# Forming the first chunk's degrees between the sums of the first source tiles of layer 1

## The chip, the cores and the metric

The kernel runs on one core of a Trainium2 chip. The metric is the device time of one execution in microseconds (us). Engines: PE is TensorE's matmul, PEld its weight load, DVE VectorE, ACT ScalarE, POOL GpSimd, SP SyncE, which here only issues DMAs.

## The reference

Four layers of a graph network over 3125 nodes and 50000 edges, with a layer norm and a relu ahead and the input added at the end. Each layer averages over a node's incoming edges; the divisor is the node's degree, at least one.

```python
def _sage_conv(x, src, dst, Wl, Wr, b):
    agg = jax.ops.segment_sum(x[src], dst, num_segments=n)
    deg = jax.ops.segment_sum(jnp.ones_like(dst, dtype=x.dtype), dst, num_segments=n)
    mean = agg / jnp.maximum(deg, 1.0)[:, None]
    return mean @ Wl + x @ Wr + b
h = jnp.maximum(_layernorm(x, axis=-1), 0.0)
h = jax.nn.relu(_sage_conv(h, src, dst, Wl1, Wr1, b1))
h = jax.nn.relu(_sage_conv(h, src, dst, Wl2, Wr2, b2))
h = jax.nn.relu(_sage_conv(h, src, dst, Wl3, Wr3, b3))
return x + _sage_conv(h, src, dst, Wl4, Wr4, b4)
```

## The kernel before

**The matrix of edge counts.** The sum over edges is a product with a matrix `counts`: row = source node, column = destination node, value = how many edges join them. It stays in SBUF as 25 source tiles (NT) of 128 rows, in f16. The destinations are worked through in 7 chunks (NCH), six of 512 nodes (4 tiles each, TPC) and one of 53. `ORDER` begins with chunk 5, then the chunk of 53, then 4, 3, 2, 1, 0. "q" is the place in that order, so q = 0 is chunk 5.

**How the matrix is made.** It is built during the kernel. A *step* is one product of PE (`step`, L2183) of two one-hot tables, which adds up to 128 edges to a window of destinations in PSUM (`window_ps`). DVE makes the tables in *groups*: for windows of 8 nodes, three steps to a group, with two instructions each (L1479); for the narrower windows of 4 nodes four steps to a group, one instruction (L1472). There is room for three groups; DVE reuses the oldest when PE is through with it. When a pair of windows is full ACT copies it to `counts` (L1876), and the next window that wants the bank waits for that copy (`window_stored`). Before layer 1 begins the matrix holds chunk 5 only. The rest is made between layer 1's sums.

**Layer 1's place q = 0.** The list `script(0)` gives the order in which PE, DVE and ACT go through this place: for each of the 25 source tiles k a first half of the sum ("sum"), then a second half ("half"), and after each half two or three steps. A half is two products of 512 columns (`add_sources`, L2362), one for the high and one for the low part of the sources. On every engine other work hangs on the numbers k in a table called `first_round`: on DVE the moments, shifts and low parts of the layer norm of the chunks still to come (`h0_moments`, `h0_shift`, `h0_low_part`) and tables of edges (`bases_late`, `late_rows`); on PE the transposes of normalized inputs (`h0_turn(j)`, L2128) and their product with Wr1 (`own_products(j)`, L2140), both through the PSUM banks `lin_ps`; on ACT the roots and the copies. Each engine runs its own list in order, and semaphores join them.

**The degrees.** Ahead of the first half PE forms the degrees of chunk 5 (`add_degrees(0)`, L2384): for each of its 4 tiles of destinations, 25 products of `counts` (as weights, 128 x 128) with two columns of ones, 100 in all, into eight columns of `lin_ps`. DVE then takes the maximum with one and the reciprocal (`degrees(0)`, L1616 and L1618), and `degree_inverted` tells PE that these columns have been read. `h0_turn(2)`, PE's first use of `lin_ps` after that, waits for it; PE issues it ahead of source tile 4. The turned degrees are used after tile 24. Place q = 2 forms its 100 products in the same way, ahead of its sums (L2384 too).

**The start of q = 0.** PE comes to it from the last steps of chunk 5 once ACT has copied the last window, after a loop over windows with unusually many edges (`heavy_of`). DVE comes to it from the same loop and first does `h0_moments(3)` and `bases_late(2)`, which hang on tile 0, and then the first two groups of tables. SP waits for the first product of the first sum (`chunk_begun`) and then issues a small copy within SBUF and the stores of the turned inputs.

Of the kernel before, what the change touches and what calls it, by code (L numbers as in the profile page):

```python
# [26 lines left out]
def sage_stack_kernel(nc, x, src, dst, Wl1, Wr1, b1, Wl2, Wr2, b2, Wl3, Wr3, b3, Wl4, Wr4, b4, out):  # L27
# [14 lines left out]
    P = 128  # L42
# [3 lines left out]
    NT = -(-N // P)  # L46
    TAIL = N - (NT - 1) * P
    TPC = 4
# [59 lines left out]
    ORDER = [NFULL - 1, NFULL] + list(range(NFULL - 2, -1, -1))  # L108
# [59 lines left out]
    for at_, (w, i) in enumerate(STEP):  # L168
        if i:
            continue  # L170
        k = STEPS[w]
# [8 lines left out]
    BY_STEPS = 3  # L180
# [87 lines left out]
    with ctx:  # L268
# [10 lines left out]
        counts = sb("counts", [P, NT, NPAD], f16)  # L279
# [77 lines left out]
        ones16 = upper[:, NWIN:NWIN + P]  # L357
# [139 lines left out]
        lin_ps = pb("lin_ps", [P, 2, 512], f32)  # L497
# [70 lines left out]
        own_copied = sem("own_copied")  # L568
# [9 lines left out]
        degree_done = sem("degree_done")  # L578
# [142 lines left out]

        assert len(FILLS[-1]) == 32 and BY_STEPS == 3
        IN_LIN = 5
        FIRST_J, FILL_J = 3, 2
        LAST_DEGREE_TURN_K = 22
        H0_LATE_K, OWN_LATE_K = 1, (4, 5)
# [441 lines left out]
        def _(dve):  # L1168
# [29 lines left out]
            def h0_moments(j):  # L1198
                c = ORDER[j]
                n, t = size_of(c)  # L1200
                dve.wait_ge(x_loaded[c], 16 if n == CH else 32)
                if j > 0:
                    dve.wait_ge(moments_made, BEFORE[j])
                for i in range(t):
                    order.after(v.bn_stats(stats[:, i, :], x_in[c][:, i, :])) if i == t - 1 else v.bn_stats(
                        stats[:, i, :], x_in[c][:, i, :])
                for i in range(t):
                    v.bn_aggr(moments[c][:, i, :], stats[:, i, :]).then_inc(moments_made, 1)
# [16 lines left out]
            def h0_low_part(j):  # L1225
                c = ORDER[j]
                n, t = size_of(c)
                tiles = slice(c * TPC, c * TPC + t)
                dve.wait_ge(h0_high, j + 1)
                if n == CH:  # L1230
                    v.scalar_tensor_tensor(out=H[:, tiles, 1, :], in0=x_in[c][:, 0:t, :], scalar=0.0,
                                           in1=H[:, tiles, 0, :], op0=ALU.max, op1=ALU.subtract).then_inc(h0_low, 1)
                else:
                    twin = slice(TWIN, P)
                    v.scalar_tensor_tensor(out=H[twin, tiles, 0, :], in0=x_in[c][twin, 0:t, :], scalar=0.0,
                                           in1=H[twin, tiles, 0, :], op0=ALU.max, op1=ALU.subtract).then_inc(h0_low, 1)
# [29 lines left out]
            def bases_late(piece):  # L1266
                if piece == 2:
                    dve.wait_ge(lo_made, 3)
                bases(piece, base_late[piece - 2], PIECES[piece][0])
                if piece == 3:  # L1270
                    dve.sem_inc(bases_made, 1)
# [340 lines left out]
            def degrees(q):  # L1612
                n, t = size_of(chunk_at(q))
                rows_ = P if n == CH else n
                dve.wait_ge(degree_done, q + 1)
                order.after(v.tensor_scalar(rdeg_columns[0:rows_, q, 0:t], lin_ps[0:rows_, 0, 0:2 * t].rearrange(  # L1616
                    "p (t a) -> p t a", a=2)[:, :, 0], 1.0, None, ALU.max))
                v.reciprocal(rdeg_columns[0:rows_, q, 0:t], rdeg_columns[0:rows_, q, 0:t]).then_inc(degree_inverted, 1)  # L1618
# [7 lines left out]
            for i, w in enumerate(FILLS[-1]):  # L1626
                if i in between:
                    between[i]()
                for j in range(steps_of([w])):
# [1 line left out]
            load_heavy(dve, regs, 0)  # L1631
            dve.wait_ge(consts_made, CONSTS)
            heavy_of(-1)
            first_round = {0: lambda: (h0_moments(3), bases_late(2)), 1: lambda: (degrees(0), h0_low_part(2)),
                           3: lambda: bases_late(3), 5: lambda: (late_rows(), h0_shift(3)), 7: lambda: h0_shift(4),
                           9: lambda: h0_low_part(3), 10: lambda: square_weights(), 11: lambda: late_tables(2),
                           12: lambda: h0_low_part(4), 13: lambda: h0_shift(5), 15: lambda: h0_low_part(5),
# [419 lines left out]
        def _(pe):  # L2057
# [292 lines left out]
            def add_sources(l, q, bank, k, first, final, halves=None):  # L2350

                c = chunk_at(q)
                n, t = size_of(c)
                if l == 1:
                    k = TILES[k]
                rows_, parts = (STACK, 1) if k == NT - 1 else (P, 2)
                if l == 1 and k == NT - 1:
                    pe.wait_ge(tail_doubled, 16 * (q + 1))
                tile = H_tiles(l, k, 1)[0:rows_, 0, :, :]
                for h in halves or range(AGG[l]):  # L2360
                    for part in range(parts):
                        last = m((agg_ps, window_ps)[bank][:, h, 0:n], tile[:, part, h * P:(h + 1) * P],  # L2362
                                 counts[0:rows_, k, chunk_cols(c, n)], start=first and part == 0,
                                 stop=final and part == parts - 1)
                        if l == 1 and first and h == 0 and part == 0:
                            last.then_inc(chunk_begun, 1)
                    if final:
                        last.then_inc(agg_done[l], 1)

            def add_degrees(q):  # L2370

                c = chunk_at(q)
                n, t = size_of(c)
                rows_ = P if n == CH else n
                if q == 0:
                    pe.wait_ge(own_copied, 2 * FILL_J)
                elif q == 1:
                    pe.wait_ge(own_copied, 2 * IN_LIN)
                else:
                    pe.wait_ge(low_done[1], q - 1)  # L2380
                for i in range(t):
                    for k in range(NT):
                        of = slice(0, TAIL if k == NT - 1 else P)
                        last = m(lin_ps[0:rows_, 0, 2 * i:2 * i + 2], counts[of, k, bass.ds((c * TPC + i) * P, rows_)],  # L2384
                                 ones16[of, 0:2], start=(k == 0), stop=(k == NT - 1))
                last.then_inc(degree_done, 1)

            def sum_cuts(q):

# [55 lines left out]
            for q in range(NCH):  # L2445

                if q == 2:
                    load_heavy(pe, regs, 1)
                    pe.wait_ge(step_tables, 5)
                pe.wait_ge(window_stored, filled_after(q - 1))  # L2450
                if q < BY_STEPS:
                    add_degrees(q)
                else:
                    if q < NCH - 1:
                        sum_cuts(q)
                    pe.wait_ge(low_done[1], q - 1)
                for kind, k in script(q):
                    if kind == "step":
                        step(*k)
                    if kind == "half":  # L2460
                        if k == 0 and q >= 1:
                            pe.wait_ge(agg_scaled[1], 2 * q)
                        add_sources(1, q, 0, k, k == 0, k == NT - 1, halves=(1,))
                    if kind == "lin":
                        lin_part(q - 1, k)
                    if kind == "narrow":
                        narrow_part(q - 1, k)
                    if kind != "sum":
                        continue
                    if k == 2 and 0 < q < BY_STEPS:  # L2470
                        pe.wait_ge(degree_inverted, q + 1)
                    if k == CUT_SUM_K and q == NCH - 1:
                        sum_cuts(q)
                    if q == 0 and k in LOW_AT:
                        pe.wait_ge(h0_low, LOW_AT[k])
                    if q == 0 and k in first_round:
                        first_round[k]()
                    if q == 1 and k == H0_LATE_K:
                        for j in range(IN_LIN + 1, NCH):
                            h0_turn(j)  # L2480
                    if q == 1 and k in OWN_LATE_K:
                        own_products(IN_LIN + OWN_LATE_K.index(k))
                    if q == 1 and k == TURN_K:
                        pe.wait_ge(own_copied, 2 * NCH)
                    if k == 0 and q >= 1:
                        pe.wait_ge(agg_scaled[1], 2 * q - 1)
                    add_sources(1, q, 0, k, k == 0, k == NT - 1, halves=(0,))
                    if k == (NT, LAST_DEGREE_TURN_K, DEGREE_TURN_K, NT, NT, NT, NT)[q]:
                        turn_degrees(q)
                    if q >= 1 and k == TURN_K:  # L2490
                        turn(1, q - 1, 0)
                if q == 0:
                    pe.wait_ge(rdeg_made, 1)
                    pe.wait_ge(norms_made, 3)
                    h0_turn(IN_LIN)
                heavy_of(q)
# [105 lines left out]
```

## Time and profile before

| | |
|---|---|
| median of 3 executions | 645.88 us (645.56 to 646.54) |
| profiled execution, its own time | 645.63 us |
| its span, first to last instruction | 643.8 us |
| outside the span | 1.8 us |
| PE busy | 615.5 us, 96% of the span |
| DVE busy | 318.9 us, 50% |
| ACT busy | 194.1 us, 30% |
| mean granted clock of TensorE | 0.986 of full |

Times inside the profile count from the span's start. A granted clock of 1.00 is the upper of TensorE's two levels, 2.4 GHz, and 0.50 the lower, 1.2 GHz. PE busy has to be read with care: it is also "busy" while its products run at the lower level.

### The profile page before, as it was taken

What the parts mean: (1) busy time and instruction counts of PE and PEld (TensorE: products, weight loads), DVE (VectorE), ACT (ScalarE), POOL (GpSimd) and SP (SyncE); (2) the same over time, 40 slices, a digit from 0 to 9 for tenths busy, and PEclk for the clock granted to TensorE, in tenths of its full rate; (3) what the DMA queues carried; (4) which work ended last, traced back from release to release, by engine and by line L of the source; (5) the groups of instructions that cost most, each with busy time, mean ns of one, the idle gap of its engine ahead of it and who ended that gap; (6) DMA issues with size and microseconds to landing.
All of it is one profiled execution on the core that took longest, in us unless ns stands there. A gap on an engine that the chain in (4) does not pass through costs nothing.

```text
span 643.8 us, 10273 instructions
## 1 busy us (share of the span) xinstructions
PE 615.5 (96%) x4155; PEld 339.3 (53%) x4156; DVE 318.9 (50%) x616; ACT 194.1 (30%) x411; POOL 41.8 (6%) x91
## 2 busy tenths in 40 slices
PE   5678999999999999999999999999999999999998
PEld 4435555656555555554444445444445646556586
DVE  6977876878888779721211111111126343334421
ACT  3876866365653622300111001122122010000100
POOL 8001300000000000000000000000002020110110
PEclk9977999999999999999999999999999999999999
DMA  8401200510210202142433531534451133030330
GB/s 265 104 1 46 85 1 3 184 57 6 68 53 15 88 23 83 34 139 67 147 89 89 151 86 50 106 98 111 140 126 33 43 86 113 2 115 10 105 116 33
DMA packets 59687, 51.00 MB, mean 79 GB/s; under 512 B 31670, under 2 KB 44507, under 8 KB 59640
## 3 DMA queue, kind: packets, MB, share of 16 engines
q1 hardware_dynamic: 59284, 49.74, 26.8%
q8 instruction: 33, 0.54, 0.3%
q0 software_dynamic: 240, 0.37, 0.2%
q10 hardware_dynamic: 116, 0.24, 0.1%
q14 instruction: 14, 0.11, 0.1%
HBM read 28.15 MB, written 16.60 MB: 70 GB/s over the span
## 4 chain that ended last, share of the span: by engine, by line
PE 86%; DVE 6%; ACT 3%; DMA 2%; issue 2%; POOL 1%; SPq 0%; DVEq 0%; ACTq 0%; POOLq 0%
PE agg_ps L2362 34%; PE window_ps L2362 19%; PE lin_ps L2297 5%; PE window_ps L2183 5%; PE lin_ps L2246 3%; PE lin_ps L2140 2%; PE agg_ps L2338 2%; PE lin_ps L2266 2%; PE lin_ps L2305 2%; DVE early L1479 1%; PE lin_ps L2384 1%; PE degree_ps L2061 1%; PE turn_ps L2183 1%; PE window_ps L2338 1%; ACT counts L1876 1%
## 5 line engine op out<-in xcount | busy, mean ns | idle before, releaser
L2362 PE MATMUL agg_ps<-counts,H 128*128 128x512 f16 (+2 forms) x1026 | 235.1, 355 | 1.0 <-DVE aggT L1570 0.8
L2362 PEld LDWEIGHTS agg_ps<-counts,H 128*128 128x128 f16 (+1 forms) x1026 | 79.2, 98 | 56.2 <-issue 10.2
L1876 ACT ACTIVATE counts<-window_ps 128x400 f16<-128x400 f32 x150 | 73.5, 506 | 62.8 <-PE window_ps L2183 49.7
L1472 DVE TENSOR_TENSOR counts<-early 128x2048 f16<-128x2048 bf16 x66 | 78.0, 1213 | 7.2 <-PE window_ps L2183 4.8
L2362 PE MATMUL window_ps<-counts,early 128*128 128x512 f16 (+2 forms) x346 | 77.8, 379 | 0.0
L2362 PEld LDWEIGHTS window_ps<-counts,early 128*128 128x128 f16 (+1 forms) x346 | 33.5, 98 | 41.3 <-issue 3.4
L2362 PE MATMUL window_ps<-counts,H 128*128 128x512 f16 (+1 forms) x291 | 55.2, 346 | 0.0
L2183 PEld LDWEIGHTS window_ps<-counts 128*128 128x128 f16 x412 | 30.9, 99 | 33.2 <-issue 4.6
L1472 DVE TENSOR_TENSOR early<-early 128x1024 f16<-128x1024 bf16 (+1 forms) x69 | 43.9, 684 | 7.6 <-PE window_ps L2183 6.1
L2362 PE MATMUL agg_ps<-counts,early 128*128 (+4 forms) x297 | 46.5, 314 | 0.0
L2183 PE MATMUL window_ps<-counts 128*128 128x100 f16 x412 | 41.4, 210 | 1.0 <-DVE counts L1472 0.8
L1926 ACT ACTIVATE newT<-newT,columns 128x512 f32<-128x512 f32 (+1 forms) x21 | 13.4, 663 | 90.6 <-DVE newT L1754 66.2
L1134 POOL TENSOR_TENSOR newH<-newH,plan 128x256 f32<-128x256 f32 (+1 forms) x25 | 18.3, 760 | 334.2 <-DMA newH<-in_x_dram 334.2
L2183 PE MATMUL window_ps<-early 128*128 128x100 f16 (+1 forms) x256 | 33.1, 229 | 7.0 <-DVE early L1479 5.3
L2362 PEld LDWEIGHTS window_ps<-counts,H 128*128 128x128 f16 x291 | 24.7, 97 | 28.6 <-issue 1.1
L2183 PEld LDWEIGHTS window_ps<-early 128*128 128x128 f16 x256 | 21.7, 102 | 33.7 <-ACT counts L1876 6.9
L1570 DVE SCALAR_TENSOR_TENSOR aggT<-agg_ps,columns,rdeg 128x512 f32<-128x512 f32 (+1 forms) x21 | 13.7, 679 | 46.5 <-PE agg_ps L2362 43.4
L2362 PEld LDWEIGHTS agg_ps<-counts,early 128*128 128x128 f16 (+1 forms) x297 | 22.0, 97 | 24.3 <-issue 1.1
L1923 ACT ACTIVATE newT<-lin_ps,columns 128x512 f32<-128x512 f32 (+1 forms) x14 | 10.1, 723 | 66.8 <-PE lin_ps L2297 62.5
L2039 ACT ACTIVATE H<-selfT 128x512 f16<-128x512 f32 (+1 forms) x12 | 6.1, 557 | 70.5 <-DMA selfT<-hT_d 70.5
L1591 DVE SCALAR_TENSOR_TENSOR partsT<-newT,partsT 128x512 f16<-128x512 f32 (+1 forms) x9 | 5.3, 587 | 44.1 <-ACT partsT L1940 43.9
L2246 PE MATMUL lin_ps<-aggT,W 128*128 128x512 f32 (+1 forms) x56 | 25.1, 564 | 0.6 <-DVE aggT L1570 0.6
(302 smaller groups left out, 712.5 us busy)
## 6 DMA issues: line engine op xcount, KB each, us to landing
selfT<-hT_d SPq DMA_DIRECT2D x18, 512.0 KB, 4.2
hT_d<-newT SPq DMA_DIRECT2D x12, 512.0 KB, 4.6
rdeg<-rdeg_d SPq DMA_DIRECT2D x22, 256.0 KB, 4.1
counts<-in_x_dram SPq DMA_DIRECT2D x6, 512.0 KB, 8.1
hT_d<-counts SPq DMA_DIRECT2D x6, 512.0 KB, 3.6
newH<-in_x_dram SPq DMA_DIRECT2D x6, 512.0 KB
out_dram<-newT SPq DMA_DIRECT2D x5, 512.0 KB
hT_d<-newT SPq DMA_DIRECT2D x6, 256.0 KB, 3.8
```

The costliest lines, as they stand in the source:

```text
L1134: nc.gpsimd.tensor_tensor(x4[0:q, i, :], x4[0:q, i, :], b4rows[0:q, :], ALU.add).then_inc(x4_biased, 1)
L1472: v.tensor_tensor(hots_of(group).rearrange("p r a (n d) -> p r a n d", d=2), pairs.unsqueeze(1).unsqueeze(1).broadcast_to([P, n, 2, P // 2 ...
L1570: v.scalar_tensor_tensor(out=aggT[:, h, 0:n], in0=(agg_ps, window_ps)[bank][:, h, 0:n], scalar=SPLIT if l == 4 else unscale[:, l - 1:l], i ...
L1876: a.activation(counts[:, :, 2 * w * WIN:2 * (w + 1) * WIN].rearrange("p t (a w) -> p a t w", a=2), window_bank(FILL_AT[w])[:, 0:2 * KEYS]. ...
L1926: a.activation(newT[:, h, 0:n], source, ACT.Relu, bias=bT[:, bias + h:bias + h + 1]).then_inc(relu_done[l], 1)
L2140: last = m(h0_ps(j)[h][:, 0:n], W14[:, 1, k, h * P:(h + 1) * P], x_T[c][:, k, 0:n], start=(k == 0), stop=(k == 1))
L2183: m(window_bank(at)[:, key0:key0 + keys], one_src, one_key, start=(j == 0), stop=(j == STEPS[w] - 1)).then_inc(hot_used, 1)
L2246: last = m(lin_ps[:, h, 0:n], W14[:, 0, k, h * P:(h + 1) * P], aggT[:, k, 0:n], start=(k == 0), stop=(k == 1))
L2266: m(last_ps(i)[0:rows_, 0:D], h, w, start=(j == 0), stop=(j == len(products) - 1))
L2297: last = m(lin_ps[:, h, 0:n], w, r, start=(i == 0), stop=(i == len(ops) - 1))
L2338: last = m((agg_ps, window_ps)[bank][:, h, cols], tile[:, part, h * P:(h + 1) * P], counts[0:rows_, k, c * CH + g * HALF_CH:c * CH + (g + ...
L2362: last = m((agg_ps, window_ps)[bank][:, h, 0:n], tile[:, part, h * P:(h + 1) * P], counts[0:rows_, k, chunk_cols(c, n)], start=first and p ...
```

## The change

The 100 products of chunk 5's degrees no longer stand ahead of the first sum. Each of the first eight halves of sums (source tiles 0 to 3, two halves each) is followed by 13 of them (the eighth by the last 9), ahead of that half's steps. They are the same products into the same columns in the same order. The wait for `own_copied` moves with them, behind the first half. On DVE `degrees(0)` moves from tile 1 to tile 4, since its inputs are complete only after tile 3. `add_degrees` for q = 1 and q = 2 is as before.

```diff
+        FIRST_DEGREES = 13
...
-            first_round = {0: lambda: (h0_moments(3), bases_late(2)), 1: lambda: (degrees(0), h0_low_part(2)),
+            first_round = {0: lambda: (h0_moments(3), bases_late(2)), 1: lambda: h0_low_part(2), 4: lambda: degrees(0),
...
-                if q == 0:
-                    pe.wait_ge(own_copied, 2 * FILL_J)
-                elif q == 1:
+                if q == 1:
                     pe.wait_ge(own_copied, 2 * IN_LIN)
...
+            def add_first_degrees(slot):
+
+                c = ORDER[0]
+                if slot == 0:
+                    pe.wait_ge(own_copied, 2 * FILL_J)
+                for at in range(FIRST_DEGREES * slot, min(FIRST_DEGREES * (slot + 1), TPC * NT)):
+                    i, k = at // NT, at % NT
+                    of = slice(0, TAIL if k == NT - 1 else P)
+                    last = m(lin_ps[:, 0, 2 * i:2 * i + 2], counts[of, k, bass.ds((c * TPC + i) * P, P)],
+                             ones16[of, 0:2], start=(k == 0), stop=(k == NT - 1))
+                    if at == TPC * NT - 1:
+                        last.then_inc(degree_done, 1)
...
-                if q < BY_STEPS:
+                if 0 < q < BY_STEPS:
                     add_degrees(q)
-                else:
+                elif q > 0:
...
                         add_sources(1, q, 0, k, k == 0, k == NT - 1, halves=(1,))
+                        if q == 0:
+                            add_first_degrees(2 * k + 1)
...
                     add_sources(1, q, 0, k, k == 0, k == NT - 1, halves=(0,))
+                    if q == 0:
+                        add_first_degrees(2 * k)
```

Lines of the changed kernel are numbered 2 higher from DVE's part on (13 to 17 higher after the new function's place). The next rows are PE's program at the start of q = 0 before the change; `lin_ps<-newH,counts 128x2` are the degrees' products (`newH` holds the ones), `agg_ps` a half of a sum, `window_ps` the steps.

```order
L2236 ISA
L2384 MATMUL lin_ps<-newH,counts 128x2 x100
L2362 MATMUL agg_ps<-counts,H 128x512 x2
L2183 MATMUL window_ps<-early 128x200 x3
L2362 MATMUL agg_ps<-counts,H 128x512 x2
L2183 MATMUL window_ps<-early 128x200 x2
```

And the same place in the changed kernel:

```order
L2238 ISA
L2364 MATMUL agg_ps<-counts,H 128x512 x2
L2396 MATMUL lin_ps<-newH,counts 128x2 x13
L2185 MATMUL window_ps<-early 128x200 x3
L2364 MATMUL agg_ps<-counts,H 128x512 x2
L2396 MATMUL lin_ps<-newH,counts 128x2 x13
L2185 MATMUL window_ps<-early 128x200 x2
```

Between PE's arrival and its first three steps there stood 100 small products and one half of a sum; now there stand 13 and one half.

The end of the products in the changed kernel, ahead of `h0_turn(2)` (L2130, eight transposes into `lin_ps`), on PE:

```order
L2364 MATMUL agg_ps<-counts,H 128x512 x2
L2396 MATMUL lin_ps<-newH,counts 128x2 x9
L2185 MATMUL window_ps<-early 128x100 x2
L2130 MATMUL lin_ps<-newH,counts 128x128 x8
L2364 MATMUL agg_ps<-counts,H 128x512 x2
```

Before, tile 3 ended with the same half, steps and transposes without the 9 products between them.

DVE's program before the change, from the second group of tables on (L1231 is `h0_low_part(2)`, L1276 `late_rows`, L1222 the last part of `h0_shift(3)`; the ten small instructions of `bases_late(3)`, L1250, stand between the third and fourth of the blocks here and are left out):

```order
L1479 TENSOR_TENSOR early<-early 128x600
L1616 TENSOR_SCALAR newH<-lin_ps 128x4
L1618 RECIPROCAL newH<-newH 128x4
L1231 SCALAR_TENSOR_TENSOR H<-counts,H 128x4x256
...
L1472 TENSOR_TENSOR early<-early 128x1024 x2
L1276 TENSOR_SCALAR counts<-degree_ps 128x6
```

In the changed kernel, the two pieces that answer to these:

```order
L1481 TENSOR_TENSOR early<-early 128x600
L1233 SCALAR_TENSOR_TENSOR H<-counts,H 128x4x256
...
L1474 TENSOR_TENSOR early<-early 128x1024
L1618 TENSOR_SCALAR newH<-lin_ps 128x4
L1620 RECIPROCAL newH<-newH 128x4
L1474 TENSOR_TENSOR early<-early 128x1024
L1278 TENSOR_SCALAR counts<-degree_ps 128x6
```

The two instructions of `degrees(0)` now stand behind `bases_late(3)` and one group of tables, with the next group, `late_rows` and `h0_shift(3)` queued behind them. The programs of ACT, POOL and SP are unchanged.

## Rows read from the trace of the kernel before

**Rows 1.** The page: span, and each engine's busy time
```profile
span 643.8 us, 10273 instructions
PE 615.5 (96%) x4155; PEld 339.3 (53%) x4156; DVE 318.9 (50%) x616; ACT 194.1 (30%) x411; POOL 41.8 (6%) x91
```

**Rows 2.** The chain that ended last: start us, us, what
```profile
49.83 0.77 issue
50.60 3.30 PE lin_ps L2384 x100
53.90 0.97 PE agg_ps L2362 x2
54.87 0.50 PE window_ps L2183 x3
...
61.25 0.43 PE agg_ps L2362 x2
61.77 0.89 PE lin_ps L2128 x8
```

**Rows 3.** Granted clock by windows (PEclk stands third from the end)
```profile
52.00:53.00 1.00, 1.00 (x33) 0.94 (x30) 1.00 (x4) 0.58 (x2) 0.00 (x0) 0.80 0.00 0
53.00:54.00 1.00, 1.00 (x27) 0.93 (x27) 0.23 (x2) 0.14 (x1) 0.00 (x0) 0.50 0.00 0
...
59.00:60.00 1.00, 1.00 (x6) 0.44 (x5) 0.85 (x5) 0.23 (x1) 0.00 (x0) 0.79 0.15 41
```

**Rows 4.** The degrees' products alone, two windows at either clock
```profile
51.00:51.50 0.50, 0.50 (x20) 0.47 (x17) 1.00 0.00 0
53.00:53.50 0.50, 0.50 (x20) 0.50 (x20) 0.50 0.00 0
```

**Rows 5.** DVE's timeline: start us, us, instruction [idle before <-releaser]
```profile
50.97 0.77 DVE L1250 TENSOR_TENSOR counts<-counts 98x128 f16<-98x128 f16 x5
51.78 1.39 DVE L1479 TENSOR_TENSOR early<-early 128x384 f16<-128x384 bf16 x4
53.94 0.16 DVE L1616 TENSOR_SCALAR newH<-lin_ps 128x4 f32<-128x4 f32 x1 [0.77 <-PE lin_ps L2384]
54.23 1.19 DVE L1231 SCALAR_TENSOR_TENSOR H<-counts,H 128x1024 f16<-128x1024 f32 x1
...
60.72 0.16 DVE L1276 TENSOR_SCALAR counts<-degree_ps 128x6 int32<-128x6 f32 x1
...
61.20 1.38 DVE L1222 TENSOR_SCALAR counts<-counts,newH 128x256 f32<-128x256 f32 x4
62.50 1.93 DVE L1472 TENSOR_TENSOR early<-early 128x1024 f16<-128x1024 bf16 x3
```

**Rows 6.** PE's timeline before, at and after the degrees
```profile
48.29 0.34 PE L2183 MATMUL agg_ps<-early 128*128 128x200 f16 x2 [0.29 <-ACT counts L1876]
...
61.60 1.06 PE L2128 MATMUL lin_ps<-newH,counts 128*128 128x128 f32 x8
...
63.97 0.30 PE L2183 MATMUL window_ps<-early 128*128 128x100 f16 x3
```

**Rows 7.** ACT's timeline at the start of q = 0
```profile
53.85 0.30 ACT L1824 ACTIVATE newH<-counts 128x4 f32<-128x4 f32 x1 [1.27 <-issue]
55.24 0.50 ACT L1876 ACTIVATE counts<-window_ps 128x400 f16<-128x400 f32 x1 [1.09 <-PE window_ps L2183]
```

**Rows 8.** PE's timeline: the same products at place q = 2
```profile
124.14 3.22 PE L2384 MATMUL lin_ps<-newH,counts 128*128 128x2 f16 x100
```

**Rows 9.** Granted clock behind those products, as in rows 3
```profile
127.00:128.00 1.00, 1.00 (x16) 0.59 (x13) 0.97 (x6) 0.00 (x0) 0.00 (x0) 0.84 0.66 131
...
131.00:132.00 1.00, 1.00 (x11) 0.63 (x10) 0.00 (x0) 0.68 (x2) 0.00 (x0) 0.95 0.11 30
```

**Rows 10.** The edge tables' gathers (POOL) and PE's first use of them
```profile
61.77 1.18 POOL L1119 DMA_INDIRECT counts<-edge_rows,counts  x1 [46.83 <-DVE counts L1276]
...
71.67 0.32 PE L2090 MATMUL degree_ps<-ident,counts 128*128 128x128 f16 x3
```

More of the change, by code:

```diff
@@ L723, in sage_stack_kernel @@
         IN_LIN = 5
+        FIRST_DEGREES = 13
+        assert 8 * FIRST_DEGREES >= TPC * NT
         FIRST_J, FILL_J = 3, 2
```

## The prediction

> **What bounds the kernel now.** I read the page first: PE is busy 96% of the span, every other engine half of it or less [rows 1]. So what counts is what PE does without working, and at which clock it works. Then the chain that ended last, from the arrival at q = 0 on [rows 2]: it runs through PE alone. PE starts the 100 small products at 50.60, needs 3.30 us, and goes from there to sums, steps and the transposes of `h0_turn(2)` at 61.77 (the chain dates a matmul's end a little later than the timeline, which has them at 61.60 [rows 6]). No wait for another engine stands between. Third, the granted clock [rows 3]: PE was idle from 48.6 (the end of the last step, 48.29 and 0.34 [rows 6]) to 50.6, then had two us of two-column products, and at about 52.6 the clock went to the lower level (0.80 over the window 52 to 53). It came back at about 59.4 (0.79 over 59 to 60). From 53.9 to 59.3, 5.4 us, the sums and steps ran at half speed, which costs half of that, 2.7 us.
>
> Last the lists of the engines that PE will meet earlier: DVE [rows 5] and ACT [rows 7]. DVE is the important one. Until 51.74 it makes `bases_late(2)`, from 51.78 to 53.17 the first two groups of tables. Today nobody notices, since PE wants the first group only at 54.66, behind the products and half a sum.
>
> **The change part by part.** *The products themselves.* 100 in 3.30 us is 33 ns each [rows 2]. They take the same at either clock: a half us at 1.00 and one at 0.50 hold the same count, 20 with those cut by its edges [rows 4]. So PE's work on them stays 3.3 us, 0.42 us for 13. Nothing is removed. The first load of weights in each slot can go beside the sum ahead of it, but the step behind the slot loses the same cover, since two columns hide nothing; I take the net as nothing. The trace has no such mixture; the bounds are eight loads more or fewer, 8 x 33 ns = 0.26 us either way.
>
> The Trainium skill, "TensorE: Matmul & The Clock Gate", section "Step-by-step: what each phase is for", says that weights for the next product are loaded while the present one runs. By that alone the eight slots would save 0.26 us; the same rule takes it back at the step behind, which had that cover before.
>
> *Wait 1, the first tables.* The sum's first half now starts at 50.60, at the full clock, 0.43 us (a later half at full clock, 61.25 [rows 2]). With 13 products PE is at its first step at 51.45. The tables are four instructions in 1.39 us from 51.78, so the first group is there at 52.48 [rows 5], whatever PE does: what stands ahead of it on DVE doesn't wait for the sums. PE waits 1.05 us. Behind that wait stands everything PE has. The wait was covered by the 87 products that have gone.
>
> *Wait 2, the copy.* ACT is occupied until 54.15 with the root of `h0_root(3)` (53.85 and 0.30, after 1.27 us without a releaser) and only then copies the first windows, 0.50 us [rows 7]. The third pair of windows, five steps in, needs that bank: PE comes to it at about 54.4, the copy is done at 54.7. 0.25 us.
>
> *Wait 3, the reciprocals.* `h0_turn(2)` needs `degrees(0)`, and DVE can begin it only at product 100, which is now two steps ahead of the transposes. Maximum and reciprocal take from 53.90 to about 54.3 [rows 2, 5]: 0.4 us, of which the steps cover 0.09. I take 0.35 us. Before, the transposes came seven us later.
>
> *Wait 4, what is queued behind `degrees(0)`.* DVE has a group of tables (0.64 us), `late_rows` and the small instructions of the shift (60.72 to 61.20, 0.48), the shift (61.20 to 62.50, 1.30) and then the group for the 24th step (0.64) [rows 5], in all 3.06 us from the reciprocal. Before, DVE began this before PE got to the transposes. PE wants that group 63.97 - 61.60 = 2.37 us after the start of the transposes [rows 6], which is at the reciprocal too. 0.7 us, and with the semaphores 0.75.
>
> Together 1.05 + 0.25 + 0.35 + 0.75 = 2.4 us. Above that I see nothing late: the product of layer 1's own weights behind gives DVE 3.5 us to catch up. The gathers on POOL wait for `late_rows` (L1276), so they start some 2 us later too, but 61.77 to 71.67 is far more than they need ahead of PE's use of them, and PE's use moves with them [rows 10]. SP's copy and stores wait for the first product of the sum and come 3.3 us earlier; no wait in the chain here is for them.
>
> *What the clock gives back.* The small products don't slow down at the lower clock, so it pays to have them there. PE's two us of idleness before 50.6 remain and it does even less up to 52.5, so I expect the fall at about 52.6 again. If the clock returns at 59.3 as before, the 6.7 us between hold four slots of products (52 x 33 ns = 1.7 us) and wait 2 (0.25), and 4.75 us of sums and steps instead of 5.4. That is 0.65 us less at half speed: 0.3 us back. The first half sum at full clock is within this.
>
> **Sum:** 2.4 - 0.3 = +2.1 us on the profiled execution's own 645.63, which is 647.7. The median of the runs shown stands 0.25 us above that execution, so a median could as well be 647.9; I keep 647.7.
>
> **The rivals.** *The clock returns early.* Mixed products, steps and sums may be enough for an earlier return. The nearest rows: at q = 2 it fell at 127.7, at the end of 3.2 us of small products, and was back at 131.0 after 3.4 us of sums and steps [rows 8, 9]. If it is back at 56.0, 3.4 us after its fall, only 3.4 - 0.25 - 0.85 = 2.3 us of sums and steps are slow, 3.1 less than before, 1.55 us saved: +0.85, 646.5. Against it: at q = 0 it took from 52.6 to 59.4 [rows 3], with small products only at the beginning; now they are all along.
>
> *The clock returns late.* It may not return at all while small products are mixed in: at the lower clock they are a quarter of PE's time (0.42 beside 0.85 of sum and 0.17 to 0.50 of steps). Then PE crawls through all of them, to about 64.1, and needs 3.4 us of dense work after it as at q = 2 [rows 8, 9], so returns at 67.5. Between 52.6 and 67.5 lie 14.9 - 0.6 (waits 2 and 3) - 2.8 (87 products) = 11.5 us of slow work against 5.4, 3.05 us more. Wait 4 goes, because a slow PE lets DVE catch up: 1.65 + 3.05 = +4.7, 650.3. For it: both returns in the rows came only after 3.4 to 5.4 us with nothing but sums and steps.
>
> *The clock doesn't fall, so that the kernel is not slower.* The half sum at 50.6 now stands in the stretch that ended in the fall. If that and the mixture behind it keep the clock up, all 2.7 us of slow work are saved against 2.4 us of waits: -0.3, 645.3. It decides at a price of 2.4: at most 0.6 us of slow work may be left. Against it: PE idles from 48.6 to 50.6 and again, by wait 1, from 51.45 to 52.5; only 0.43 us of dense work stand between.
>
> The Trainium skill's same page, section "What's actually happening", says of the monitor behind the clock that it is free-running and "doesn't reset when your kernel starts". By that, executions of one kernel would differ in where the clock falls and returns, and a median mixes the cases above. The one trace here can't show it; the three times lie 1 us apart, which would fit.
>
> *The waits aren't there.* For this DVE would have to reach the tables sooner. Its first row here starts when PE's loop is over, as before, so I see no way.
>
> **How the numbers follow.** A measurement of this kernel can tell 0.2%, 1.3 us, from no change: slower begins at 647.2, faster ends at 644.6. Waits with a return between 57 and 61: 0.50, between +1.4 and +2.9 (647.0 to 648.5; the 0.26 of either sign is in it). Early return: 0.20, 646.3 to 647.0. Late return: 0.22, 649.3 to 650.6. Clock stays up: 0.06, 645.0 to 645.9. Something else that makes it faster: 0.02. The likeliest is the first, 647.7, its own range 647.0 to 648.5. For 8 in 10 I leave out the upper half of the late return and the cases with the clock up: 646.3 to 650.0. Slower by over 0.2%: 0.45 of the first and the late return, 0.67. Same: the rest of the first, the early return, the clock that stays up: 0.30. Faster: 0.03.
>
> **What would show it.** Wait 1: PE's first three steps wait for DVE's L1481 for about 1 us, to 52.5. Wait 3: `h0_turn(2)` waits for L1620. Wait 4: PE's next steps wait for L1474 for 0.7 us. The products: 13 in about 0.42 us, and the steps behind them without a gap. The clock: its windows between 52 and 68 say which case it is. If PE has no wait at 51.5, or the steps behind the slots start late by more than a weight load, or the clock keeps its full level, the prediction is wrong in that step. Behind 75 us everything should be shifted as a whole.

## The result

The changed kernel takes 652.59 us in the median of 4 executions (651.32 to 653.73), the kernel before 646.21 us beside it on the same chip (4 executions, 645.56 to 647.79). The ratio is 1.0102, with a 95% interval of 1.0077 to 1.0126: slower by 6.4 us. Forecast were 647.7, with 646.3 to 650.0 as the range for 8 in 10. The direction was right; two thirds of the loss were not foreseen.

The page of the changed kernel, profiled in an execution of 651.32 us (lines of the changed kernel are numbered 2 higher than in rows 1 to 10 up to `add_sources`, L2364; the degrees' products are now L2396):

```profile
span 649.5 us, 10273 instructions
PE 618.6 (95%) x4155; PEld 341.6 (53%) x4156; DVE 319.0 (49%) x616; ACT 194.1 (30%) x411; POOL 42.4 (7%) x91
```

PE is busy 3.1 us longer with the same 4155 products than in [rows 1], and has 2.6 us more time without any.

**Where the time lies.** All three engines load the list of windows with many edges (`heavy`) into registers just ahead of q = 0, and again at q = 2. The two loads cut the kernel into three parts. One row for each kernel, of before and of after: engine, operation, count, duration in ns (lowest, middle, highest), start of the first and of the last in us.

```profile
L1154 DVEq TENSOR_LOAD <-heavy x2: 981/985/989, 47.6 to 123.3; - x2
```

```profile
L1156 DVEq TENSOR_LOAD <-heavy x2: 976/984/993, 47.4 to 128.8; - x2
```

Between the loads lie 75.7 us before and 81.4 after, 5.7 more. Ahead of the first there are 47.6 and 47.4, behind the second 520.5 and 520.7 of the spans. So in these two profiles everything happened in the stretch with the change, and nothing was given back or lost later. I call this stretch M and quote it for every experiment, since it leaves out the part ahead of the first load, which took between 47.4 and 49.4 us in the profiled executions, whatever the edit. A fall of the clock behind the degrees' products of q = 2 lies behind M.

PE's timeline after, from its arrival on (idle time before, and its releaser, in brackets):

```profile
50.48 0.59 PE L2364 MATMUL agg_ps<-counts,H 128*128 128x512 f16 x2 [2.05 <-ACT counts L1878]
50.91 0.47 PE L2396 MATMUL lin_ps<-newH,counts 128*128 128x2 f16 x13
52.47 0.66 PE L2185 MATMUL window_ps<-early 128*128 128x200 f16 x3 [1.09 <-DVE early L1481]
52.92 1.06 PE L2364 MATMUL agg_ps<-counts,H 128*128 128x512 f16 x2
53.77 0.71 PE L2396 MATMUL lin_ps<-newH,counts 128*128 128x2 f16 x13
54.34 0.33 PE L2185 MATMUL window_ps<-early 128*128 128x200 f16 x1
56.48 0.35 PE L2185 MATMUL window_ps<-early 128*128 128x200 f16 x1 [1.81 <-ACT counts L1878]
...
64.32 0.45 PE L2396 MATMUL lin_ps<-newH,counts 128*128 128x2 f16 x9
64.70 0.26 PE L2185 MATMUL window_ps<-early 128*128 128x100 f16 x2
65.44 1.92 PE L2130 MATMUL lin_ps<-newH,counts 128*128 128x128 f32 x8 [0.48 <-DVE newH L1620]
...
69.48 0.29 PE L2185 MATMUL window_ps<-early 128*128 128x100 f16 x3
```

There are three waits, 1.09 + 1.81 + 0.48 = 3.38 us. The second is the one that was put at 0.25. Its history is in the chain that ended last (start, us, what; "ACTq" is ACT's sequencer, which handles register instructions):

```profile
52.21 0.19 ACT counts L1817
52.40 0.02 issue
52.42 2.97 ACTq L1156
...
55.73 0.30 ACT newH L1826
56.03 0.40 ACT counts L1878
56.43 0.05 issue
56.48 0.35 PE window_ps L2185
```

Before, the chain went through PE alone here [rows 2]. Now it goes through ACT, and in ACT through one register load, L1156 (L1154 before). The same load in the two kernels, on ACT:

```profile
L1154 ACTq TENSOR_LOAD <-heavy x2: 902/908/914, 52.6 to 123.7; - x2
```

```profile
L1156 ACTq TENSOR_LOAD <-heavy x2: 919/1944/2968, 52.4 to 129.3; - x2
```

It begins at about the same time but takes 2.97 us in place of 0.90; the one at q = 2 still takes 0.92. What has moved beside it are SP's DMAs. Before:

```profile
54.47 0.68 SPq L858 DMA_DIRECT2D counts<-counts  x1
55.20 1.27 SPq L812 DMA_DIRECT2D hT_d<-counts  x2
```

After, with the windows of their transfers (the last two columns are the DMA engines' busy share and GB/s, the one ahead of them the granted clock):

```profile
50.89 0.68 SPq L860 DMA_DIRECT2D counts<-counts  x1
51.62 1.27 SPq L814 DMA_DIRECT2D hT_d<-counts  x2
```

```profile
52.00:53.00 1.00, 0.53 (x4) 0.51 (x5) 1.00 (x4) 0.40 (x2) 0.00 (x0) 0.50 0.10 26
53.00:54.00 1.00, 1.00 (x10) 0.44 (x9) 1.00 (x1) 0.00 (x0) 0.00 (x0) 0.50 0.83 298
54.00:55.00 1.00, 0.67 (x13) 0.39 (x10) 1.00 (x4) 0.00 (x0) 0.00 (x0) 0.50 0.77 254
```

SP is released by the first product of the first sum. That product no longer has 100 small ones ahead of it, so the stores start 3.6 us sooner and lie in the middle of ACT's load. Behind the load ACT has the root of `h0_root(3)` (55.73, before 53.85 [rows 7]) and the first copy of windows, for whose bank PE waits.

**The clock.** It fell at about 51.8 (0.91 over the window 51 to 52), came back at 62.0, and fell once more from 65.5 to 68.9, behind the wait for the reciprocals. Before it was low once in this stretch, from 52.6 to 59.4 [rows 3]: 6.8 us then, 13.6 now.

```profile
51.00:52.00 1.00, 0.38 (x14) 0.29 (x12) 0.96 (x7) 0.94 (x5) 0.00 (x0) 0.91 0.00 0
...
62.00:63.00 1.00, 1.00 (x23) 0.87 (x22) 0.00 (x0) 0.97 (x4) 0.00 (x0) 0.97 0.00 0
...
65.00:66.00 1.00, 0.56 (x3) 0.59 (x4) 0.96 (x5) 0.50 (x1) 0.00 (x0) 0.74 0.00 0
...
68.00:69.00 1.00, 1.00 (x6) 0.51 (x5) 0.74 (x2) 0.00 (x0) 0.80 (x1) 0.56 0.29 66
```

Of the 13.6 us, 0.7 are the end of wait 1, 1.8 wait 2, and 1.6 are four slots of small products, which don't care. The other 9.5 us were sums, steps and transposes at half speed, against 5.4 before: 4.1 more, half of which is 2.05 us. Waits of 3.4 us and 2.05 us of slower work make 5.45 of the 5.7 us of M; 0.25 us are left for everything else, the joints of the slots among it.

### The profile page after: what moved, and what is told of

Same layout as the page of the kernel before. It is cut to its first block, busy times and chain, and to the rows that moved or that the text cites. A ratio compares the mean times of both kernels' runs of the same rounds, so it can differ in the third digit from the quotient of the medians.

```text
span 649.5 us, 10273 instructions
## 1 busy us (share of the span) xinstructions
PE 618.6 (95%) x4155; PEld 341.6 (53%) x4156; DVE 319.0 (49%) x616; ACT 194.1 (30%) x411; POOL 42.4 (7%) x91
## 4 chain that ended last, share of the span: by engine, by line
PE 85%; DVE 6%; ACT 3%; DMA 2%; issue 2%; POOL 1%; ACTq 0%; SPq 0%; DVEq 0%; POOLq 0%
PE agg_ps L2364 34%; PE window_ps L2364 19%; PE lin_ps L2299 5%; PE window_ps L2185 5%; PE lin_ps L2248 3%; PE lin_ps L2142 2%; PE agg_ps L2340 2%; PE lin_ps L2268 2%; PE lin_ps L2307 1%; PE turn_ps L2185 1%; DVE early L1481 1%; PE degree_ps L2063 1%; PE window_ps L2340 1%; ACT counts L1878 1%; PE lin_ps L2270 1%
## 5 line engine op out<-in xcount | busy, mean ns | idle before, releaser
L2364 PE MATMUL agg_ps<-counts,H 128*128 128x512 f16 (+2 forms) x1026 | 236.2, 356 | 3.0 <-ACT counts L1878 2.0
L2364 PEld LDWEIGHTS agg_ps<-counts,H 128*128 128x128 f16 (+1 forms) x1026 | 79.3, 99 | 58.5 <-issue 12.4
L2364 PE MATMUL window_ps<-counts,early 128*128 128x512 f16 (+2 forms) x346 | 77.7, 379 | 0.0
L2364 PEld LDWEIGHTS window_ps<-counts,early 128*128 128x128 f16 (+1 forms) x346 | 33.5, 98 | 41.2 <-issue 3.4
L2364 PE MATMUL window_ps<-counts,H 128*128 128x512 f16 (+1 forms) x291 | 55.2, 346 | 0.0
L2364 PE MATMUL agg_ps<-counts,early 128*128 (+4 forms) x297 | 46.5, 314 | 0.0
L2364 PEld LDWEIGHTS window_ps<-counts,H 128*128 128x128 f16 x291 | 24.7, 97 | 28.6 <-issue 1.1
L2364 PEld LDWEIGHTS agg_ps<-counts,early 128*128 128x128 f16 (+1 forms) x297 | 22.1, 97 | 24.3 <-issue 1.1
```

## The experiments

"Held" in what follows means: the changed kernel with the edit of e1. My theory was that the stores beside ACT's load cost most of what was not foreseen; the rivals were that the waits for tables and reciprocals, or the clock alone, do it. Numbers of before beside the experiments: 646.35 (e1 to e4), 645.74 (e5 to e8), 646.29 us (e9 to e12), 15 or 29 executions each.

**e1: after, with SP held until ACT's fourth root.**

```diff
                 if l == 1:
+                    sp.wait_ge(root_made, 4)
                     double_tail(0)
```

> The changed kernel, and SP waits for ACT's root of chunk place 3 before it issues its copy and stores of q = 0, so they come after ACT's register load instead of beside it. Theory A (the stores, started 3.6 us earlier by the change, slow ACT's register load from 0.9 to 3.0 us, and PE waits 1.8 us for ACT's copy): the load is back at 0.9 to 1.0 us, PE's wait for the copy falls from 1.8 to at most 0.4 us, and the time is 1.4 to 2.5 us under the changed kernel's. Theory B (the load is slow for another reason, PE's or DVE's earlier work): the load stays near 3 us, the time within 0.5 us of the changed kernel's.

Measured: 647.95 us (12 executions), ratio 1.0031 [1.0014, 1.0048]. 4.6 of the 6.4 us are gone, more than the 1.4 to 2.5 expected, which counted the wait and left out the clock. M is 77.5. PE's waits, and ACT's root (lines one higher again):

```profile
52.51 0.66 PE L2186 MATMUL window_ps<-early 128*128 128x200 f16 x3 [1.16 <-DVE early L1482]
62.95 1.06 PE L2131 MATMUL lin_ps<-newH,counts 128*128 128x128 f32 x8 [0.48 <-DVE newH L1621]
65.79 0.29 PE L2186 MATMUL window_ps<-early 128*128 128x100 f16 x3 [0.31 <-DVE early L1475]
```

```profile
53.70 0.30 ACT L1827 ACTIVATE newH<-counts 128x4 f32<-128x4 f32 x1 [1.27 <-issue]
```

The wait for ACT isn't there, the root is back in its place, and the low clock is 6.8 us as before (51.9 to 58.7). What is left is what had been forecast: waits of 1.16, 0.48 and 0.31 us, and a time near 647.7. One of the twelve executions took 652.09 us, with a mean clock of 0.979 against 0.987 to 0.989 in the others.

**e2: before, with SP released by the first product of the degrees** (the collision without the change). It drops the release behind the first sum of q = 0 and adds:

```diff
+                        if q == 0 and i == 0 and k == 0:
+                            last.then_inc(chunk_begun, 1)
```

> The kernel before, but SP is let go by the first of the 100 degree products instead of the first product of the sum, 3.3 us earlier, as in the changed kernel; nothing else moves. Theory A: ACT's register load takes 2.5 to 3 us here too; ACT then copies the first pair of windows at 56.0 to 56.5 instead of 55.2, PE waits up to 0.5 us for it, and the time is 0 to 1 us over before. Theory B: the load stays at 0.9 us, no change.

Measured: 646.62 us (12), ratio 1.0001 [0.9989, 1.0012], M 75.9. ACT's load took 3.08 us, and PE waited 0.39:

```profile
L1154 ACTq TENSOR_LOAD <-heavy x2: 892/1984/3076, 54.0 to 125.3; - x2
```

```profile
58.14 0.35 PE L2183 MATMUL window_ps<-early 128*128 128x200 f16 x1 [0.39 <-ACT counts L1876]
```

So the slow load comes from the stores and not from the changed order of PE. With 100 products ahead of the sum it lies almost wholly under PE's work and costs nothing that can be measured. The collision costs time only together with the change's loss of cover.

**e3: after, with two slots of 50 products** (`FIRST_DEGREES = 50`).

> The changed kernel with 50 products behind each of the first two halves instead of 13 behind each of eight. Theory A with the waits of the prediction: the 50 products take 1.6 us and cover the wait for the first tables (1.1 us) and most of the wait for ACT's copy (1.8 us to at most 0.5), the waits at the reciprocals (0.5 us) go as well, and there is no second fall of the clock: 4 to 6 us under the changed kernel, about the kernel before (within 1 us). A rival: the interleaving as such costs (slots of products run slower than in one piece, the clock falls whenever they stand between sums): then at most half of the 6 us comes back.

Measured: 647.61 us (12), ratio 1.0017 [1.0005, 1.0029], M 77.2. The 37 products more ahead of the first steps cover wait 1 whole; the load still takes 2.98 us, PE waits 0.64 for ACT. 5.0 us came back, as expected, but the median is 1.3 over before and not within 1. The clock didn't fall a second time, as expected, but it was low for 10.2 us against 6.8 before, and for 6.8 against 3.4 at q = 2, in the profile.

**e4: after, with `bases_late(2)` on DVE behind the first tables** (the wait for tables removed alone).

```diff
-            first_round = {0: lambda: (h0_moments(3), bases_late(2)), 1: lambda: h0_low_part(2), 4: lambda: degrees(0),
+            first_round = {0: lambda: h0_moments(3), 1: lambda: (bases_late(2), h0_low_part(2)), 4: lambda: degrees(0),
```

> The changed kernel, with bases_late(2) on DVE moved from tile 0 to tile 1, behind the first two groups of tables. The wait of PE for the first tables falls from 1.1 to 0.3 us. If waits add up, the time falls by 0.7 us. If ACT's copy is what PE waits for next whatever the tables do (ACT is held until 56.0 by its register load), PE only waits 0.8 us longer there and the time stays within 0.3 us of the changed kernel's; I expect this.

Measured: 653.91 us (6), ratio 1.0103 [1.0084, 1.0122], M 82.4, with low clock for 17.1 us in the profile against 13.6 in after: nothing gained.

```profile
53.59 0.42 PE L2185 MATMUL window_ps<-early 128*128 128x200 f16 x3 [0.33 <-DVE early L1481]
58.48 0.35 PE L2185 MATMUL window_ps<-early 128*128 128x200 f16 x1 [3.36 <-ACT counts L1878]
```

The wait for tables shrank to 0.33 us and the wait for ACT grew from 1.81 to 3.36: PE only came sooner to the same late copy. While the load is slow, no cost of wait 1 shows.

**e5: held, with two slots of 50** (e1 and e3 together).

> The changed kernel with both: SP's copy and stores held until ACT's root, and 50 products behind each of the first two halves. If the two remedies are for different waits (theory A), PE has no wait left between 50.5 and 70 and the time is 0.3 to 1.5 us under two slots alone, within 0.5 us of the kernel before. If holding the stores only helps because it shortens a stretch that two slots shorten too, the time equals two slots alone.

Measured: 646.68 us (11), ratio 1.0004 [0.9992, 1.0017]. No wait of PE between its first sum and `own_products(2)`, low clock 6.8 us, M 75.5 against 75.7. The change is back at the time of before once both covers are.

**e6: after, with the small copy early and only the stores held.**

```diff
                     double_tail(0)
+                    sp.wait_ge(root_made, 4)
                     for j in range(3):
```

> The changed kernel, SP's small copy within SBUF (53 KB) as early as there, but the three stores behind it held until ACT's root. If the big stores are what slows ACT's register load, the load takes 0.9 to 1.2 us and the time is that of the kernel with both held (1.3 to 2 us over before). If the small copy does it, the load stays at 3 us and the time at 6 us over before. I expect the first.

Measured: 652.03 us (4), ratio 1.009 [1.0058, 1.0121].

```profile
L1157 ACTq TENSOR_LOAD <-heavy x2: 902/1086/1271, 54.1 to 131.0; - x2
```

The load took 1.27 us and PE's wait for ACT's copy is 0.3 us, so it is the two stores (512 and 53 KB) that make the load slow; the load beside the copy within SBUF alone (53 KB) was 0.37 us longer than before's 0.90. The time stayed high all the same, and the expectation, which had it lower, was missed there: the clock was low for 17.1 us in the profile (54.1 to 71.2), and M is 81.4. The mean clocks of the four were 0.989 (648.2 us), 0.982 (651.4), 0.976 (652.7) and 0.979 (653.1). The execution at the high clock is at e1's time, the others at that of after. So a load that is nearly quick again is not enough to bring the time back; the clock has to return early too.

**e7: held, four slots of 25.**

> The changed kernel, copy and stores held, 25 products behind each of the first four halves. The products end at tile 1, so the waits for the reciprocals (0.5 us) and for the tables behind them (0.3 us) go, and the first tables are waited for 0.75 instead of 1.15 us. By the waits alone: 1.2 us under the kernel with the stores held and thirteen to a slot, that is 0.4 us over the kernel before. If mixing products with sums costs by itself, by the clock, it stays 1 us or more over before.

Measured: 649.73 us (5), ratio 1.0067 [1.0053, 1.0081], M 77.5. A wait for the tables of 0.78 us, as expected, and low clock of 10.2 us at q = 0 with 6.8 at q = 2 where before has 3.4. By the waits it should have been 0.4 us over before; it is 4.0 over, so here the rival came true: the clock costs what the waits give back. All five executions had a mean clock of 0.981 or 0.982.

**e8: held, the first steps one source tile later**, with `h0_low_part(2)` on DVE behind them (`FIRST_STEPS_K = 1`).

> The changed kernel, copy and stores held, and the steps of q = 0 begin at tile 1 instead of tile 0, with h0_low_part(2) on DVE at tile 2. PE has 1.7 us of sums and products before it needs the first tables, so wait 1 (1.15 us) falls to under 0.3 us. Waits 3 and 4 stay or grow by 0.3 us. If waits add up: 0.8 to 1.1 us under the kernel with the stores held. If the clock, low in either, hides it: under 0.4 us.

Measured: 653.38 us (4), ratio 1.0126 [1.0111, 1.0142], M 81.9. It should have been about 1 us under e1 and is 5.4 over it. Wait 1 was gone, but steps that begin a tile later come more to a half, and PE waited for copies (1.31 and 0.43 us) and later for tables (1.33); the clock was low for 10.2 us. It moves waits and says nothing about the theory.

**e9: after, with ACT's load moved ahead of the last windows of chunk 5**; the stores stay early.

```diff
             for i, w in enumerate(FILLS[-1]):
+                if i == len(FILLS[-1]) - 2:
+                    load_heavy(act, regs, 0)
...
-            load_heavy(act, regs, 0)
             heavy_of(-1)
```

> The changed kernel with SP's stores as early as there, but ACT's register load moved ahead of its last two copies of chunk 5, where ACT stands idle and no store runs. If the collision of load and stores is the cause, the 3 us go without touching SP: PE's wait for ACT's copy falls from 1.8 to at most 0.3 us and the time is that of the kernel with the stores held (647 to 649). If it was the stores themselves, through what they do to other engines, the time stays at 651 or more.

Measured: 647.44 us (12), ratio 1.0019 [1.0008, 1.003]. The load is at 47.7 and takes 0.90 us, and 5.2 us are gone with the stores where the change puts them. With e1 and e2 this shows the collision from both sides: either partner may be moved, and PE's wait for ACT's copy goes. The profiled execution was the slowest of the twelve (648.93 us) and the only one with a mean clock of 0.982, the others had 0.987 to 0.989; it has the waits of 1.15 and 0.39 us and no wait for ACT.

```profile
L1156 DVEq TENSOR_LOAD <-heavy x2: 971/979/987, 47.4 to 128.5; - x2
```

M is 81.1, nearly that of after, without wait 2: the clock was low for 17.1 us, from 52.0 to 69.0. Some 2 us came back behind M (518.6 us against 520.7 in after), where the clock didn't fall at q = 2. Up to 57 us, PE's rows in this profile lie 0.03 to 0.04 us ahead of e1's, with the same products in the same order. Where the clock returned in e1, and here:

```profile
58.00:59.00 1.00, 1.00 (x15) 0.46 (x13) 0.73 (x2) 0.00 (x0) 0.00 (x0) 0.65 0.17 54
```

```profile
69.00:70.00 1.00, 1.00 (x10) 0.55 (x9) 0.93 (x4) 1.00 (x3) 0.90 (x1) 0.98 0.24 66
```

So nearly the same work on PE was followed by a return at 58.7 in one execution and at 69.0 in the other.

**e10: e9's edit with two slots of 50.**

> The load sooner on ACT and 50 products behind each of the first two halves: the best mixture so far with the collision gone. No wait between 50.5 and 70, clock low for 6.8 us: 0 to 1 us under the kernel before, most likely no difference that can be measured.

Measured: 645.44 us (12), ratio 0.9989 [0.9976, 1.0002]; no wait in the same stretch as in e5, low clock 6.8 us, M 75.5. It is the best of all and still not clear of no change. PE's first slots:

```profile
52.27 0.59 PE L2365 MATMUL agg_ps<-counts,H 128*128 128x512 f16 x2 [1.98 <-ACT counts L1878]
52.70 1.64 PE L2397 MATMUL lin_ps<-newH,counts 128*128 128x2 f16 x50
54.33 0.66 PE L2186 MATMUL window_ps<-early 128*128 128x200 f16 x3
```

**e11: held, with 8 of the 100 products** (those with k = 0 and k = 24).

```diff
+                    if k not in (0, NT - 1):
+                        continue
```

> The changed kernel with copy and stores held, and 92 of the 100 products left out (only the first and last source tile of each degree group are formed, so the degrees of chunk 5 are incomplete). PE then has sums and steps alone and no products mixed in. If the mixture is what keeps the clock low, the low stretch at 52 is 6.8 us in every execution and the time is 3 us (the products) under the kernel with the stores held, in every execution, with a spread under 2.5 us. If the clock is low for other reasons, some executions are 3 to 5 us longer, as there.

Measured: 647.03 us (10), ratio 1.001 [0.9996, 1.0023], M 74.9. With 92 products less, 3.0 us of PE's work, the stretch is 0.8 us shorter than before and 2.6 shorter than in e1: PE waits 1.45, 0.47 and 0.30 us, and low clock is 3.4 us. By this kernel, of the 3.0 us that these products take in before, 2.2 us are time in which PE would otherwise wait. Against e1, where they cover little, M fell by nearly all of their time, but the median by 0.9 us and not by the 3 expected of a kernel in which the mixture keeps the clock low. The mean clocks were 0.984 to 0.989, the times within 2.3 us.

**e12: held, with each product formed twice** (the second into another bank of `lin_ps`).

```diff
+                    m(lin_ps[:, 1, 2 * i:2 * i + 2], counts[of, k, bass.ds((c * TPC + i) * P, P)],
+                      ones16[of, 0:2], start=(k == 0), stop=(k == NT - 1))
```

> The changed kernel with copy and stores held, and each of the 100 products formed twice (the second into columns of lin_ps that nobody reads), so 26 behind each half. By PE's work alone it costs 3.3 us, less 0.4 at the tables' wait: 651. If more small products between the sums hold the clock low, the low stretch lasts through all the slots, some 16 us or more, in every execution, and the time is 654 or above, mean clock at or under 0.980.

Measured: 652.87 us (4), ratio 1.0108 [1.008, 1.0135]. Whether small products as such keep the clock down is not settled by this: with twice as many of them it was low for 3.4 us in the profile (54.5 to 57.9), with a mean clock of 0.990, and another execution had 0.989 (651.1 us); the other two had 0.979, at 653.6 and 654.3 us, as the rival had it for all. So they don't do it in every execution. M is 78.6, 1.1 more than in e1. The profiled spans of e12 and e1 are 4.3 us apart, of which 1.1 are in M and 1.3 behind it; 1.9 lie in the part ahead of the first load, where the kernels are the same.

## Why the prediction was wrong

**The step that failed** is in the part on what follows the four waits: "SP's copy and stores wait for the first product of the sum and come 3.3 us earlier; no wait in the chain here is for them". They do come earlier, 3.6 us. I looked only for instructions that wait for them. They run beside ACT's register load, which then takes 2.97 us instead of 0.90 (which part of the chip the two share is not shown), and that load stands ahead of a root and a copy for which PE waits. The 1.27 us "without a releaser" ahead of the root, named in wait 2, were mostly this load; I took them as fixed. With that, **wait 2** was mis-sized: 1.81 us for 0.25. Taking it away by e1 or e9 brings 647.95 and 647.44, within the likeliest case's own range.

The second term that failed is the clock's. In M the sum had +2.1 us and the profile +5.7. Of the 3.6 us between them wait 2 is 1.6 and the clock 2.35 (slow work cost 2.05 us more than before, and 0.3 us were to come back); waits 1 and 3 were 0.17 us longer than forecast, wait 4's 0.75 us did not come, and 0.25 us have no name.

**Wait 1** was right: 1.09 us for 1.05. But e4 shows that with a wait 2 of this size it can't be added as the sum did. They stand in a row, and what PE doesn't wait for tables it waits for ACT.

**Wait 3** was right in place and somewhat larger: 0.48 us for 0.35. **Wait 4** isn't there in after, where PE runs late and slow and lets DVE catch up, as the case of the late return had said; at the earlier return in e1 it is 0.31 us for 0.75.

**The products.** The last six slots stand in the chain of after with 0.32, 0.51, 0.33, 0.47, 0.30 and (nine products) 0.30 us, of which these are two:

```profile
57.68 0.32 PE lin_ps L2396 x13
...
59.21 0.51 PE lin_ps L2396 x13
```

That is 2.23 us for 74 products, against 2.44 at 33 ns each, a difference within the bound of 0.26 us. In the chain the steps behind them start without a gap.

**The clock.** "I expect the fall at about 52.6 again" and a return at 59.3: it fell at 51.8 and returned at 62.0, with a second fall. A late return had a chance of 0.22 with +3.05 us against before; it was worth 2.05 here. Its mechanism isn't what happened: it had the clock low through all the slots and 3.4 us beyond, to 67.5, but it returned with three slots to come, and fell again behind wait 3, which no case had. In e1, without wait 2, the return came at 58.7. So after and e1 differ in the clock as well as in wait 2, but that the one hangs on the other is not shown: e6 has 0.3 us of that wait and e9 none, and both were low for 17.1 us in the profiled execution. By the executions it is a matter of chances: the mean clock was 0.982 or less in all four of after, in three of four of e6, and in one of twelve each of e1 and e9.

The Trainium skill, "TensorE: Matmul & The Clock Gate", section "What's actually happening", calls the monitor free-running. By that rule executions of one kernel should differ, as the prediction said. The runs agree for kernels with slots of 13 (mean clock 0.987 to 0.989 in most executions of e1 and 0.979 in one, with 652.1 us); of the 73 executions of before beside e1 to e12, 72 had 0.986 or 0.987 and one 0.984, so the rule alone doesn't say in which kernel they differ.

**What stays open:** what decides when the clock returns, and with it how much of the 6.4 us hangs on the slow load beyond the wait of 1.81 us. e1 and e9 took the collision away and brought back 4.6 and 5.2 us; e6 made the load nearly quick and brought back less than 1 us. The profiles of e1 and e9 show that the order of PE's work doesn't settle it, and e7 and e12 that the number of small products in a slot doesn't either. I have no statement that fits all of them.

## What to carry to other kernels

When an edit lets an engine reach a point sooner, list every queue that this point releases, and then every transfer, register load and copy that will run at the same time, not only those that wait for it. An unexplained idle stretch ahead of an instruction ("issue" in the chain of waits) is a cost with an owner; name the owner before taking it as fixed. Small work that stands in front of a dependency may be the cheapest cover there is: here 100 products of two columns hid 1.1 us of DVE's work and, in e2, all but 0.39 us of the slow load, and splitting them freed nothing. And look at the clock of every execution, not only of the profiled one: in e9 the profiled one was the exception.

## What the runs showed of the hardware

The load of registers from SBUF ahead of q = 0 took 0.90 us on ACT in each of the nine profiles with neither copy nor stores beside it, 1.27 beside a copy of 53 KB (one profile), and 2.97 to 3.08 beside two stores of 512 and 53 KB (298 GB/s over 53 to 54 in after). ACT did nothing else meanwhile: its idle time ahead of the root was 1.27, 1.64 and 3.34 us with loads of 0.90 (before and e1), 1.27 (e6) and 2.97 (after). The Trainium skill, "DMA: Bandwidth & Descriptors", section "Latency and other measured facts", gives about 600 ns as the floor of such a load. Nearly all loads here lie above it, but the second ones of e11, at q = 2, do not: 0.56 us on ACT, 0.50 on PE's sequencer and 0.38 on DVE's. Why they were so short there is not known.

```profile
L1157 DVEq TENSOR_LOAD <-heavy x2: 378/686/993, 48.8 to 123.7; - x2
```

The mean granted clock differs between executions of some orders and not of others, at the same instructions: 0.976 to 0.989 over four executions of e6 (648.2 to 653.1 us), 0.986 to 0.987 in e10's twelve. The two orders of the changed products that leave PE no wait in this stretch (e5, e10) had the lowest medians of all kernels with the change, and mean clocks of 0.986 to 0.987 throughout.
